# Taking preparatory products out of a shared PSUM bank at the head of a step, in the attention phase of a fused kernel

## The reference

```python
def _L1_cond_ref(x, attn_bias, mask, g_in, null_attn_bias, null_kv, Wq, Wkv, Wo, g_out):
    ...
    xn = layernorm(x, g_in)
    q = (xn @ Wq).reshape(b, n, H, DH).transpose(0, 2, 1, 3) * scale
    kv = xn @ Wkv
    k, v = (kv[..., :DH], kv[..., DH:])
    ...
    k = jnp.concatenate([nk, k], axis=1)
    v = jnp.concatenate([nv, v], axis=1)
    sim = jnp.einsum('bhid,bjd->bhij', q, k)
    ...
    sim = sim + bias
    ...
    attn = jax.nn.softmax(sim, axis=-1)
    out = jnp.einsum('bhij,bjd->bhid', attn, v)
    out = out.transpose(0, 2, 1, 3).reshape(b, n, INNER)
    out = out @ Wo
    return layernorm(out, g_out)
```

## Time and profile before

| | |
|---|---|
| time, median of 3 runs | 1453.21 us (1450.84 to 1454.32) |
| profiled execution | 1449.1 us |
| its span, first to last instruction | 1447.0 us |
| TensorE busy with matmuls | 1255.0 us, 87% |
| TensorE loading weights | 998.7 us, 69% |
| VectorE busy | 1035.3 us, 72% |
| ScalarE busy | 763.9 us, 53% |
| GpSimd busy | 553.6 us, 38% |
| mean granted TensorE clock | 0.949 |

### The profile page before, as it was taken

The page is one execution under the profiler, slowest core; times in us unless marked ns, Lnnn a source line. Parts: engine busy times, 40 slices in busy tenths (PEclk is TensorE's granted clock), DMA queues, the critical chain, the costliest instruction groups (busy, mean ns, idle before and its releaser), DMA issues. The chain is left out here.

```text
span 1447.0 us, 29659 instructions
## 1 busy us (share of the span) xinstructions
PE 1255.0 (87%) x8705; PEld 998.7 (69%) x8710; DVE 1035.3 (72%) x2788; ACT 763.9 (53%) x1940; POOL 553.6 (38%) x834
## 2 busy tenths in 40 slices
PE   4999989998973699999999999999999999944866
PEld 2777877787861478778777877877787788831223
DVE  5566666656555677887887888878878878763986
ACT  3223223232221466676766767666677677624853
POOL 1333323232322576445344444454454545510014
PEclk9999999999985799999999999999999999976987
DMA  6233212210204400001000010010010000202115
GB/s 231 63 128 103 74 51 80 102 72 15 88 15 135 163 15 2 2 2 31 2 19 16 2 31 2 1 32 2 2 31 2 6 12 1 76 14 64 58 56 176
DMA packets 51039, 71.52 MB, mean 49 GB/s; under 512 B 4497, under 2 KB 43665, under 8 KB 48850
## 3 DMA queue, kind: packets, MB, share of 16 engines
q1 hardware_dynamic: 50338, 69.60, 14.4%
q10 hardware_dynamic: 560, 0.20, 0.1%
HBM read 57.07 MB, written 12.72 MB: 48 GB/s over the span
## 5 line engine op out<-in xcount | busy, mean ns | idle before, releaser
L844 POOL TENSOR_SCALAR scores<-scores,att_rinv 128x128 f32<-128x128 f32 (+3 forms) x512 | 264.2, 532 | 195.9 <-DVE att_rinv L1056 195.9
L900 ACT ACTIVATE scores<-scores,att_top 128x128 f32<-128x128 f32 (+3 forms) x512 | 281.6, 553 | 78.5 <-DVE att_top L1038 78.1
L1038 DVE CUSTOM_DVE_ANT_0 scores<-ps_y,w_bias_b,null_s 128x128 f32<-128x128 f32 x448 | 229.6, 547 | 85.3 <-PE ps_y L1188 78.9
L261 POOL TENSOR_TENSOR act_w<-act_g,wide_w 128x512 f32<-128x512 f32 x64 | 105.6, 1649 | 279.7 <-DVE act_g L379 274.1
L1187 PE MATMUL ps_y<-k_hh,q_hl 128*128 128x256 f32 (+2 forms) x512 | 190.6, 381 | 14.8 <-DVE att_top L1038 7.4
L908 ACT ACTIVATE keep<-ps_up 128x128 f32<-128x128 f32 (+3 forms) x256 | 111.9, 437 | 167.7 <-PE ps_up L1199 163.8
L1199 PE MATMUL ps_up<-ident,scores 128*128 128x128 f32 x1280 | 190.6, 274 | 9.9 <-DVE keep L1066 9.2
L208 ACT ACTIVATE hid_hi<-hid 128x512 fp32r<-128x512 f32 x80 | 50.5, 631 | 241.8 <-DVE hid L397 241.7
L1199 PEld LDWEIGHTS ps_up<-ident,scores 128*128 128x128 f32 x1280 | 150.7, 140 | 31.1 <-issue 13.0
L1210 PE MATMUL ps_a<-keep,w_val 128*64 128x128 f32 x2560 | 171.0, 281 | 0.7 <-DVE keep L1066 0.7
L851 POOL TENSOR_SCALAR w_q_hm<-q_hl 64x512 fp32r<-64x512 f32 x128 | 76.6, 611 | 227.9 <-ACT q_hl L923 227.9
(11 more groups left out here) (236 smaller groups left out, 2585.0 us busy)
## 6 DMA issues: line engine op xcount, KB each, us to landing
wide_w<-token_w_dram SPq DMA_DIRECT2D x16, 1024.0 KB, 4.6
x_raw<-in_x_t_dram SPq DMA_DIRECT2D x8, 512.0 KB, 3.8
x_nat<-in_x_nat_dram SPq DMA_DIRECT2D x8, 512.0 KB, 4.8
x_dram<-x_nat SPq DMA_DIRECT2D x8, 512.0 KB, 2.9
w_x1t<-x_dram SPq DMA_DIRECT2D x8, 512.0 KB, 4.3
c_dram<-out_raw SPq DMA_DIRECT2D x8, 512.0 KB, 3.2
c2t<-c_dram SPq DMA_DIRECT2D x8, 512.0 KB, 3.7
x_tile<-x_dram SPq DMA_DIRECT2D x8, 512.0 KB, 4.3
```

Source lines behind the costliest of these rows:

```text
L261: nc.gpsimd.tensor_tensor(act_w[:, k % 2], act_g[:, k % 2], wide_w[:, k], ALU.mult).then_inc(sem.act_w_ready, 1)
L844: nc.gpsimd.tensor_scalar(s, s, rinv[:, pp, q, hh:hh + 1], 0.0, ALU.mult, ALU.add).then_inc(sem.p_normed, 1)
L900: nc.scalar.activation(s, s, ACT.Exp, scale=-1.0, bias=top[:, pp, q, hh:hh + 1], accum_out=lsum[:, pp, q, hh:hh + 1]).then_inc(sem.exp_don ...
L1038: dve.tensor_tensor_reduce(scores_of(pp, hh, q), psS[:, hh, 0:n], bias_of(w, h)[:, CAUSAL[q]:CAUSAL[q] + n], 1.0, null_s[:, par, q, h:h + ...
```

## The change

On ScalarE and on VectorE, the instructions that take a preparatory product out of the shared bank move from the end of the step to its beginning. On VectorE `null_weights_lo`, `normed_lo` and `keys_lo` now stand ahead of the biased minimum. On ScalarE all six kinds stand ahead of the turned copy and the exponentials, and so also ahead of the two copies of `projected` in step 12. No instruction is added or taken away, and TensorE's, GpSimd's and SyncE's programs stay as they are.

```diff
--- before: ScalarE
+++ after
                 def step(b, i, par, behind, ahead):
                     n = PAIRS * b + i // 4
-                    if i % 4 == 3 and (behind or i >= 11):
-                        outputs_t(n - 2, i // 4 % 2)
-                    if i % 4 == 2 and (ahead or i < STEPS - 4):
-                        query_hi(n + 1, (i // 4 + 1) % 2)
-                    late, J, j = lagged(b, i, TLAG)
-                    if behind or not late:
-                        turned_out(J, j, group(b, i, TLAG))
-                    exps(STEPS * b + i, i)
-                    if i % 4 == 3:
-                        null_exp(n, i // 4 % 2)
-                    if behind and i == PNT + 1:
-                        null_weights(b - 1)
-                    if behind and i == OUT:
-                        projected(b - 1)
                     if ahead:
                         for c in range(HC):
                             if i == XN[c] + 1:
...
                             null_scores(b + 1)
                         if i == NT + 1:
                             null_by_token(b + 1, 1 - par)
+                    if behind and i == PNT + 1:
+                        null_weights(b - 1)
+                    if i % 4 == 3 and (behind or i >= 11):
+                        outputs_t(n - 2, i // 4 % 2)
+                    if i % 4 == 2 and (ahead or i < STEPS - 4):
+                        query_hi(n + 1, (i // 4 + 1) % 2)
+                    late, J, j = lagged(b, i, TLAG)
+                    if behind or not late:
+                        turned_out(J, j, group(b, i, TLAG))
+                    exps(STEPS * b + i, i)
+                    if i % 4 == 3:
+                        null_exp(n, i // 4 % 2)
+                    if behind and i == OUT:
+                        projected(b - 1)
--- before: VectorE
+++ after
                 def step(b, i, par, behind, ahead):
                     n = PAIRS * b + i // 4
+                    if behind and i == PNT + 1:
+                        null_weights_lo(b - 1)
+                    if ahead:
+                        for c in range(HC):
+                            if i == XN[c] + 1:
+                                normed_lo(b + 1, 1 - par, c)
+                        if i == KV + 1:
+                            keys_lo(b + 1, 1 - par)
                     biased_max(b, i, par)
...
                     if behind or not late:
                         turned_out(J, j, group(b, i, TLAG))
-                    if behind and i == PNT + 1:
-                        null_weights_lo(b - 1)
                     if behind and i in NORM_OUT:
...
                     if ahead:
                         if i in NORM_IN:
                             norm_in(b + 1, [s for s, at in enumerate(NORM_IN) if at == i])
-                        for c in range(HC):
-                            if i == XN[c] + 1:
-                                normed_lo(b + 1, 1 - par, c)
-                        if i == KV + 1:
-                            keys_lo(b + 1, 1 - par)
```

## The result

The changed kernel takes 1457.29 us (median of 7 runs, 1455.63 to 1460.18) beside 1453.21 us for the kernel before (7 runs, 1450.84 to 1455.40). The ratio is 1.0030, with a 95% interval of 1.0018 to 1.0043: 4.4 us slower, between 2.6 and 6.2 us. The forecast was 10.3 us slower. The direction is right; the size is less than half of it.

What follows compares the result with a forecast made beforehand. TensorE is busiest, but paired with VectorE step by step. Six middle batches at 1.62 us (9.7 us), batch 0 at +0.6 and batch 7 at 0 give +10.3 us: median 1463.5 us, range 1453 to 1467.5 us.

Steps and rivals of the forecast that it cites:

- Step 16, keys: VectorE idles for ScalarE's key and value copies; its shift passes through gapless work to TensorE in step 20: +1.53 us a batch.
- Steps 8 and 12, input: Taking out the input halves: first half's delay mostly absorbed, +0.05 us; second half's TensorE wait goes, -0.41 us a batch.
- Step 4, null weights: Three tiny VectorE layer norm operations fall beside GpSimd's normalising and take 1.41 us, delaying the next minimum: +0.45 us a batch.
- Batch 0: No output layer norm behind its keys, so VectorE's shift isn't passed on; TensorE's own path costs +0.6 us.
- Batch 7: Its step 4 has no layer norm of a next batch; costed at 0.
- the signs that the prediction named: Line 34's waits gone, scores waiting for minima, VectorE waiting before keys, tiny operations at 1.4 us, batch distance +1.6 us.
- the waits simply go: Rival, chance 0.10: VectorE catches up before step 20, TensorE's 11.6 us of waits at line 34 vanish, down to 1441.6 us.
- Gains and losses cancel: Rival, chance 0.15: step 16 costs 0.6 us, step 4 gives 0.3 back, -0.06 us a batch, 1453 us.
- The tiny operations don't slow down: Rival, chance 0.20: in step 4 the layer norm operations stay fast, giving 0.3 us instead of taking 0.45; 1459 us.
- The delay reaches the other queues: Rival, chance 0.08: slack of queues behind VectorE is used up, step 16 costs 2.4 us; 1468.7 us.

Runs made afterwards that it cites:

- e2: Kernel before with only the taking out of keys and values (step 16) moved to the head on both engines: 1458.75 us, ratio 1.0044.
- e7: Changed kernel with the mask row of the keys written before VectorE waits for ScalarE: 1453.96 us, ratio 1.0014 against the kernel before.
- e8: Changed kernel with a separate semaphore for ScalarE's key copies, so VectorE doesn't wait for drain and value copy: 1452.06 us, ratio 1.0000 against the kernel before.
- e10: Changed kernel with layer norm stages moved from between taking out and query product: 1442.82 us, ratio 0.9944 against the kernel before.
- e1: Kernel before with only the taking out of the input halves (steps 8 and 12) moved to the head on both engines: 1447.33 us, ratio 0.9972.
- e3: Kernel before with only the taking out of the null weights (step 4) moved to the head on both engines: 1451.61 us, ratio 1.0002.
- e5: As e3, with the input layer norm's stage of step 4 moved to step 5, and that of step 5 to step 6: 1449.65 us, ratio 0.9989.
- e6: Kernel before with only the input layer norm stages moved as in e5, nothing taken out earlier: 1452.27 us, ratio 1.0003.
- e4: Kernel before with only ScalarE taking out at the head, in all seven steps, VectorE at the end as before: 1444.40 us, ratio 0.9945.
- e9: Kernel before with ScalarE's half of the change and the layer norm stages moved as in e10: 1427.07 us, ratio 0.9835.
- e11: Kernel before with only the layer norm stages moved as in e10: 1444.63 us, ratio 0.9953.

## Why the prediction was right in its direction and wrong in its size

The prediction's six middle batches were to cost 9.7 us; they cost 5.0. What failed is the size of two terms of the sum: the input's gain in step 12, and the loss in step 4. The parts, over six batches:

- **Step 16, keys (forecast +9.2 us): right.** e2 measured +8.9 us, and batch 2 of the kernel after shows 1.53 us. The named mechanism is shown from four sides: VectorE's idle 2.06 us in the timeline; e7 and e8, which take 0.42 and 0.65 us off it and shorten the batch by about as much; e10, where the same wait costs less because VectorE has slack behind it; and batch 0, where it costs nothing. The wait of the scores of step 17 came out at 2.02 us, with 1.8 forecast. One row of it was off, and by luck another cancelled it: in batch 2 the drain ahead of the minimum was taken over at 0.37 us and takes 0.72, but from that minimum to the turned copy VectorE needs 1.32 us (731.72 to 733.04) where it needed 1.63 before (727.84 to 729.47).
- **Steps 8 and 12, input (forecast -2.2 us): the failed step, with step 4.** The text says "The whole wait of 0.41 us goes: -0.41 us, between -0.41 and 0". Measured: -0.65 us at step 12 of batch 2, and -4.4 us over six batches in e1. The mechanism is right. The size was read from the matmul's row, which shows the stall without the 0.24 us by which a matmul that isn't held starts ahead of the end of the one before; the weight load in front of it waited 0.65 us (the earlier trace rows have only the matmul's rows). Of the 4.4 us about 0.6 are the clock's, between batches 4 and 5. Step 8 costs nothing, as said: in batch 2 the minima stand 0.16 us later at step 7 and 0.17 at step 10. The lower end of this term, too, was set by the wrong row, so the range didn't hold it.
- **Step 4, null weights (forecast +2.7 us): mis-sized.** e3 measured +0.9 us. The tiny operations slow down as said, from 0.77 us up to the minimum to 1.4 us, and e5 with its control e6 shows that they are what costs. But +0.45 us was a small difference of long chains, and three starts on VectorE came earlier than I chained them. The minimum of step 4 is 0.07 us earlier, the tiny operations start 1.82 us after it in place of 1.90, and the minimum of step 5 starts 0.07 us ahead of the recorded end of the last one, in place of 0.06 behind it. Together that is 0.28 us, the whole miss.
- **The parts together** are 0.4 us less than their sum (5.4 to 5.0).
- **Batch 0 (forecast +0.6 us): 0.0.** I charged TensorE's own path; in e2 the query product comes 0.15 us late there, and by step 19 nothing of it is left. **Batch 7 (forecast 0):** about +0.3 us, its step 4.

So of the 4.7 us that the six batches miss, 2.2 are the input's term (0.6 of them the clock's), 1.8 the null weights', 0.3 the keys' and 0.4 what the sum of the parts has too much. With the batch 7 value it makes 5.3 us, or 5.8 us without the clock's share, inside the timed interval of 2.6 to 6.2 us. Of the signs that the prediction named, all came but one: the distance from one batch to the next grew by 0.83 us, not by 1.6.

Of the rivals, "the waits simply go" fell: each wait of line 34 is gone in the kernel after, which is slower, and e2 is slower still. The Trainium skill (Perfetto Trace Analysis, Optimization Strategy) tells to find the gaps of the busiest engine and let what they wait for start sooner; by that alone the time would have been 1441.6 us. The runs show where it holds here: for the input (e1, 4 us), where the minimum behind the moved work is 1.0 us late and still in time, and for ScalarE's half (e4, 6.9 us; with the layer norm stages moved as well, e9, 24 us), in which no minimum is held up. "Gains and losses cancel" (1453 us) had the wrong price of step 16 and the wrong sign of step 4; that its time lies nearer to the measured one than my forecast's is luck. "The tiny operations don't slow down" (1459 us) is nearest in time, and that too is luck: they do slow down. "The delay reaches the other queues" fell with e2.

## What to carry to other kernels

Moving a piece of work to the head of an in-order queue also moves its wait there: ask first whether the piece has anything to wait for at that place, and what else is queued behind it. Move the producer's half early and leave the consumer's half where its operand has long arrived; then clear whatever stands between that and the reader, because removing one of two late sides leaves the wait nearly as it was (6.7 us for the keys became 6.2 us in e4 and in e11). Look at the wait of the weight load, too, when you size a stall of TensorE: in step 12 it was the true size, and the matmul's was more than a third too small.

## What the runs showed of the hardware

- A stall of TensorE has two rows. For the second half of the input the matmul's row read 0.41 us and the weight load's 0.65 us, and the batch gained 0.65 us at that place when the stall was gone. The 0.24 us between them are the overlap with the transposes in front that the stalled matmul lost. For the keys the rows read 1.12 and 1.35 us, which no run tested alone; in step 4 (0.41 and 0.65 us) the gain was 0.5 us (e5 against e6).
- A tiny VectorE operation with both inputs in SBUF that began beside a GpSimd normalising instruction lasted until that instruction ended: 45 of 45 in lines 638 and 640 of the kernel after ended 5 to 13 ns behind it, at 0.28 to 0.60 us in place of 0.16.
- VectorE's explicit drain with its empty instruction, as the gap ahead of the minimum of the scores behind it, took 0.37 to 0.39 us at the end of step 16. At the head of it, it took 0.38 to 0.39 us in batches 1, 3 and 5 and 0.72 to 0.76 us in batches 2, 4 and 6 (3.4 us in six against 2.3 in the rows "DVE scores L1038 <- issue").
- In the same 13 us of batch 0, with TensorE busy all the time, one execution had a granted clock of 0.87 and another of 1.00. The 3.5 us at 0.51 within them cost about 1.6 us.
